# Local attention of a fused transformer kernel: scores as four 32-row products, values stationary, output turned beside the probabilities

## What is computed

```python
xw = x.reshape(B * nw, WINDOW, C)                      # WINDOW = 64, C = 128
qkv = (xw @ W_qkv).reshape(B * nw, WINDOW, 3, NUM_HEADS, HEAD_DIM)
q, k, v = (qkv[:, :, 0], qkv[:, :, 1], qkv[:, :, 2])
q = _layernorm(q, ln_gamma, ln_beta)                   # over the 8 features of a head
k = _layernorm(k, ln_gamma, ln_beta)
attn = jnp.einsum('bqhd,bkhd->bhqk', q * SCALE, k)     # per window and head
attn = jax.nn.softmax(attn, axis=-1)
out = jnp.einsum('bhqk,bkhd->bqhd', attn, v).reshape(B * nw, WINDOW, C)
out = out @ W_proj + b_proj
...
x = x + _L1_attn_ref(_layernorm(x, axis=-1), L1_attn_W_qkv, ...)
```

## Time and profile before

| | us |
|---|---|
| three runs | 891.72, 892.42, 892.43 |
| median | 892.42 |
| the profiled execution | 885.71 |
| its span, first to last instruction | 883.9 |
| attention stage in it, first score product to the next stage's first product | 161.4 to 323.1 |
| mean granted clock of TensorE over the span | 0.903 of full |

### The profile page before, as it was taken

One profiled execution on the slowest core, in us unless ns is written; L12 is line 12 of the kernel. 1 busy time (PEld: TensorE's weight loads), 2 busy tenths in 40 slices (PEclk: granted clock), 3 DMA queues, 4 the chain that ended last, 5 costly groups with the idle time before them and its releaser, 6 DMA issues. The chain is left out here.

```text
span 883.9 us, 11015 instructions
## 1 busy us (share of the span) xinstructions
PE 731.3 (83%) x3306; PEld 469.4 (53%) x3306; DVE 686.8 (78%) x1615; ACT 570.6 (65%) x926; POOL 394.5 (45%) x427
## 2 busy tenths in 40 slices
PE   4788998779998889999778988877778767877787
PEld 3666765445555567777566867643223222222565
DVE  6685786798998638777767888968899778786785
ACT  5264664657474435664636767667899879777776
POOL 6638665634345105555329977534323332230330
PEclk9999998988697669999969999987899889789999
DMA  4200000100000000000001000000000000000001
GB/s 134 72 12 13 16 16 18 34 24 25 13 25 19 0 1 1 1 1 0 1 0 37 1 1 0 1 0 1 1 0 1 1 1 0 1 0 1 1 1 48
DMA packets 9610, 11.59 MB, mean 13 GB/s; under 512 B 720, under 2 KB 5712, under 8 KB 9552
## 3 DMA queue, kind: packets, MB, share of 16 engines
q1 hardware_dynamic: 9552, 10.89, 4.3%
HBM read 9.84 MB, written 1.05 MB: 12 GB/s over the span
## 5 line engine op out<-in xcount | busy, mean ns | idle before, releaser
L1032 POOL TENSOR_TENSOR rbuf<-B,rbuf 128x512 fp32r<-128x512 f32 x96 | 124.1, 1295 | 83.6 <-ACT rbuf L960 83.4
L497 POOL TENSOR_SCALAR small<-small 128x4 f32<-128x4 f32 x32 | 8.5, 265 | 173.3 <-DVE small L387 172.8
L994 DVE TENSOR_TENSOR B<-B,up_banks 128x512 f32<-128x512 f32 x68 | 46.4, 683 | 42.3 <-PE up_banks L733 25.8
L945 ACT ACTIVATE B<-gate_banks 128x512 f32<-128x512 f32 x68 | 40.6, 599 | 59.4 <-PE gate_banks L733 58.3
L960 ACT ACTIVATE rbuf<-B 128x512 fp32r<-128x512 f32 x100 | 62.5, 625 | 17.3 <-DVE B L1010 12.3
L1010 DVE TENSOR_TENSOR B<-B,spread_bank 128x512 f32<-128x512 f32 x96 | 64.7, 678 | 11.0 <-ACT B L949 7.0
L1757 ACT ACTIVATE B<-B,VEC 128x1024 f32<-128x1024 f32 x48 | 55.3, 1151 | 22.4 <-DVE B L1752 22.3
L731 PE MATMUL gate_banks<-XH,WH 128*128 128x512 f32 x152 | 67.0, 441 | 0.8 <-ACT YT L1355 0.8
L733 PE MATMUL gate_banks<-XH,WL 128*128 128x512 f32 x152 | 62.4, 410 | 0.0
L732 PE MATMUL gate_banks<-XL,WH 128*128 128x512 f32 x152 | 62.3, 410 | 0.0
L949 ACT ACTIVATE B<-gate_banks,WR 128x512 f32<-128x512 f32 x64 | 44.0, 689 | 27.3 <-PE gate_banks L733 26.7
(11 more groups left out here) (347 smaller groups left out, 2274.3 us busy)
## 6 DMA issues: line engine op xcount, KB each, us to landing
STG<-in_w_split SPq DMA_DIRECT2D x27, 256.0 KB, 2.7
X<-in_x SPq DMA_DIRECT2D x4, 256.0 KB, 5.0
out<-X SPq DMA_DIRECT2D x4, 256.0 KB, 2.3
WR<-in_w_raw SPq DMA_DIRECT2D x1, 524.5 KB, 4.4
STG<-in_w_exact SPq DMA_DIRECT2D x2, 256.0 KB, 2.6
STG<-in_w_split SPq DMA_DIRECT2D x5, 64.0 KB, 1.9
STG<-in_w_split SPq DMA_DIRECT2D x1, 192.0 KB, 2.4
STG<-in_w_split SPq DMA_DIRECT2D x1, 128.0 KB, 2.0
```

Of the source, the lines that this page charges most:

```text
L994: nc.vector.tensor_tensor(MO[n % 2], AO[n % 2], U[n % 2][:, :], ALU.mult).then_inc(mul_done, 1)
L1032: e_.tensor_tensor(lo, hidden(f, n), hi.bitcast(F32), ALU.subtract).then_inc(hl_ready, 1)
```

## The change

Scores. The keys are no longer masked per tile and head. A product now reads 32 partitions, that is four heads, with keys of which each of four copies keeps every fourth head; so 4 copies (`KM`, four slots of 512 columns) serve a whole chunk, made once a chunk by `attn_keys`, which also applies gain and offset (slots 0 and 1 on ScalarE, 2 and 3 on GpSimd). A unit's scores are four products of 32 rows, 64 columns of weights and 256 streaming columns, into two banks.

Turned probabilities go back into the same two banks as the unit's scores. So the scores of unit N+1 wait for the copy-out of unit N-1.

Weighing. The values are the weights (18 columns), the turned probabilities stream (64 columns), eight products a unit, each pair of heads at its own 32 output partitions. The result comes out features by tokens; ScalarE copies it (`copy_out`), TensorE turns it by two transposes of 64 rows into free columns of the probabilities' banks (`turn_out`), and the copy-out of a later unit, widened from 512 to 640 columns, takes it along. `finish` reads it from SBUF, now once a unit.

Normalising the heads. The variances are computed with tokens on the partitions (line 1172 of the new file, eight products), root and reciprocal are of 128 x 128, ScalarE spreads them over the features (`attn_spread_act`), and TensorE turns them by full 128-row products (line 1186).

Order. TensorE now does turn(N-1) with turn_out(N-3), weigh(N-2), scores(N+1); ScalarE copy-out(N-1), copy_out(N-2), exp(N). The scores of units 0 and 1 stand inside the last feed-forward block ahead of the stage, before its last two summing triples. `body_start` is gone from the stage.

```diff
-                    i = nc.tensor.matmul(G[u][w * WIN:(w + 1) * WIN, :], QN[c_ % 2][:, tok],
-                                         KM[tile % 2][:, HU * u:HU * u + HU, w * WIN:(w + 1) * WIN],
-                                         start=True, stop=True)
...
+            if N >= 2:
+                pe.wait_ge(pt_ready, N - 1)
...
+            for w in range(2):
+                tok = slice(i_ * P + w * WIN, i_ * P + (w + 1) * WIN)
+                for k in range(2):
+                    rows = slice(32 * (2 * u + k), 32 * (2 * u + k) + 32)
+                    i = nc.tensor.matmul(SB2[u][w * WIN:(w + 1) * WIN, k, :], QN[c % 2][rows, tok],
+                                         KM[c % 2][rows, :, tok], start=True, stop=True)
...
+        def attn_keys(eng, c):
...
+            eng.wait_ge(qk_read, 2 * c + 1)
...
+            for j in ((0, 1) if eng is nc.scalar else (2, 3)):
+                dst = KM[c % 2][:, j, :]
+                if eng is nc.scalar:
+                    i = eng.activation(dst, kc, ACT.Identity, scale=key_g[:, j:j + 1], bias=key_b[:, j:j + 1])
+                else:
+                    i = eng.tensor_scalar(dst, kc, key_g[:, j:j + 1], key_b[:, j:j + 1], ALU.mult, ALU.add)
...
+            def turn_out(M):
+                u = M % 2
+                pe.wait_ge(o_copied, M + 1)
+                for k in range(2):
+                    rows = slice(64 * k, 64 * k + 64)
+                    i = nc.tensor.transpose(SBW[u][:, k, HALF:TURN_W], OT[u][rows, :], ident[rows, rows])
+                i.then_inc(o_turned, 1)
...
-                    i = nc.tensor.matmul(SP[:, pr * 36:(pr + 1) * 36], PT[u][:, q * P:(q + 1) * P],
-                                         VB[:, tile % TL, pr, :, :, :].rearrange("p a b d -> p (a b d)"),
-                                         start=True, stop=True)
...
+                        i = nc.tensor.matmul(SP[32 * q:32 * q + 2 * (HD + 1), u * P + w * WIN:u * P + (w + 1) * WIN],
+                                             VB[:, tile % TL, 4 * u + q, w, :, :].rearrange("p h d -> p (h d)"),
+                                             PT[u][:, q // 2, at_:at_ + WIN], start=True, stop=True)
...
+                a.wait_ge(o_full, N - 1)
...
+                nc.scalar.activation(PT[N % 2], SBW[N % 2][:, :, 0:TURN_W], ACT.Copy).then_inc(pt_ready, 1)
...
+            def copy_out(N):
+                u = N % 2
+                a.wait_ge(o_full, N + 1)
...
+                nc.scalar.activation(OT[u], SP[:, u * P:(u + 1) * P], ACT.Copy).then_inc(o_copied, 1)
...
             for n in range(UN):
                 N = c * UN + n
-                probs(N)
                 if N:
                     evac(N - 1)
+                if N >= 2:
+                    copy_out(N - 2)
+                probs(N)
...
+                    if f is FFN0 and at_ == (NC - 1, f.blocks - 3):
+                        for N in range(2):
+                            attn_scores(pe, N)
```

More of the change, by code:

```diff
@@ L659, in later_weights @@
         def later_weights(g, chain):
+            for row, dst in (("ln_g1", key_g), ("ln_b1", key_b)):
+                i = nc.gpsimd.tensor_scalar(dst, raw("head_of_4"), raw(row), 1.0, ALU.mult, ALU.mult)
+            chain(i)
             WM32 = buf[11]
@@ L1230, in attn_mask @@
-        def attn_mask(eng, tile):
-            c, i_ = tile // TL, tile % TL
-            if tile >= NC * TL:
-                return
-            heads, done = {nc.vector: (range(0, 8), masked_dve), nc.gpsimd: (range(8, 12), masked_pool),
-                           nc.scalar: (range(12, 16), masked_act)}[eng]
-            eng.wait_ge(qk_ready, 2 * c + 1)
-            if tile >= 2:
-                eng.wait_ge(s_full, 2 * (tile - 2) + (1 if eng is nc.vector else 2))
-            for h in heads:
-                dst, src = KM[tile % 2][:, h, :], KN[c % 2][:, i_ * P:(i_ + 1) * P]
+            if step in (4, 5):
+                k, x = step - 4, (kc, qc)[step - 4]
+                v.wait_ge(rstd_full, 2 * c + k + 1)
+                v.wait_ge(centred, 2 * c + 2)
+                nc.vector.tensor_tensor(x, x, R[:, :], ALU.mult).then_inc(qk_read, 1)
@@ new lines, in attn_prepare_dve @@
+            if step == 5:
+                v.wait_ge(qk_read, 2 * c + 2)
+                if c >= 2:
+                    v.wait_ge(s_full, UN * (c - 1))
+                nc.vector.tensor_scalar(QN[c % 2], qc, raw("ln_g1"), raw("ln_b1"), ALU.mult, ALU.add)\
+                    .then_inc(qk_ready, 1)
+        def attn_keys(eng, c):
+            if c >= NC:
+                return
+            eng.wait_ge(qk_read, 2 * c + 1)
+            if c >= 2:
+                eng.wait_ge(s_full, UN * (c - 1))
+            elif c == 1:
+                eng.wait_ge(yt_ready, count(2, 0))
+            for j in ((0, 1) if eng is nc.scalar else (2, 3)):
+                dst = KM[c % 2][:, j, :]
@@ L1360, in attn_project_dve @@
                 v.wait_ge(y_full, count_y(2, c))
+            else:
+                v.wait_ge(yt_ready, count(2, 0))
             nc.vector.tensor_copy(rbuf[0][:, :], A32w).then_inc(ah_ready, 1)
@@ L1452, in attn_dve @@
                     hook(-1)
-                attn_hooks(n, c, hook, 7)
-                if n == 5 and nxt:
-                    attn_prepare_dve(v, c + 1, 2)
+                attn_hooks(n, c, hook, 6)
+                if N >= 4:
+                    finish(N - 4)
             if not nxt:
-                finish(NU // 2 - 2)
-                finish(NU // 2 - 1)
+                for M in range(NU - 4, NU):
+                    finish(M)
                 attn_project_dve(v, c)
```

270 lines of the change are left out of this document (147 added, 123 removed).

## The result

The changed kernel takes 900.88 us (median of 4 runs, 899.31 to 902.42), the kernel before 892.31 (891.72 to 892.43): 1.0097 times, 95% interval 1.0079 to 1.0115. It is slower, where 0.7% less was forecast; 900.88 lies inside the range that the prediction gave, 870 to 903, but on the other side of no change. The profiled executions lie further apart, 900.86 against 885.71 us (spans 898.9 and 883.9): the one of before was quick for its kernel. What follows splits the 15.0 us of the two spans; the medians lie 8.6 apart.

A forecast was written before the change was run, and what follows sets the result against it. TensorE and its granted clock were taken to bound the kernel, VectorE close behind. Three chunks +4, last chunk -6, head -2.5, tail -2 sum to -6.5 us: 879.2 in profile time, forecast 886 against 892.4, range 870 to 903.

The forecast's parts named there:

- Product prices: TensorE's work per attention unit: 1.95 us against 2.46 at the upper clock level, about 3.2 against 4.7 at the lower.
- no concurrency: Rival: 18-column products run one after another, weighing takes 1.8 us, +1.1 a unit; 920 us, chance 0.06.
- The new chain: From exp to exp through turn, copy-out and result copy: 2.65 us a unit at the upper level, 3.4 at the lower.
- Side work and the lower level: Per-chunk preparation on the path: 10.5 us upper, 18 lower; whole chunk 31.7 and 45.2 against 34.2 and 48.1.
- Which clock: Attention stage's share of time at the lower level, chosen 55% against 38% now: 37.9 us a chunk, +4 for three.
- Last chunk: The last attention chunk prepares nothing, so the cheaper unit shows: 27 to 33 us against 39.9, counted as only -6.
- Head: Start of attention: scores inside the feed-forward tail wait for GpSimd's keys; -2.5 us (bounds -4 and +2), first exp near 161.5.
- Tail: From the last exp to the output's turn: 5.3 us instead of 7.5, counted as -2.
- the clock falls and stays: Rival: lower level for 85% of the stage, chunk 42.5 us, +8 in all; 900 us, chance 0.22.
- the rows argument: In the attention units, TensorE work drops by a fifth and score rows to a quarter, while the period falls by less.
- The clock holds: Rival: lower-level share stays at 38%, giving 878 us, or 860 wholly at the upper level; under 880, chance 0.22.
- hidden anyway: Rival: ScalarE's cycle takes what TensorE gives, chunks stay at 36.6 us, only the ends move; 888 to 893, chance 0.10.

The follow-up runs named there:

- e10: e7_head with each of a unit's four score products reading all 128 partitions instead of 32 (scores not the reference's); 0.9902 times the kernel before.
- e7_head: Changed kernel with values read at n=1, the projection's split ahead of the preparation step, and GpSimd's chunk 0 keys early; 0.9861 times the kernel before.
- e14_head_again: The kernel of e7_head run once more, unchanged; 0.9920 times the kernel before.
- e8_again: The changed kernel itself run once more, unchanged; 1.0066 times the kernel before.
- e2_values: Changed kernel with ScalarE's read of the value rows moved from unit n=0 back to n=1; 0.9999 times the kernel before.
- e3_valproj: e2_values with VectorE's split of the projection also put ahead of the preparation step at n=4; 0.9954 times the kernel before.
- e1_rows32: Kernel before with every score product reading only the first 32 of 128 partitions (scores not the reference's); 929.99 us, 1.0452 times the kernel before.
- e13_masked_queries: e7_head with VectorE's spread products and ScalarE's keys later, and 128-row scores from chunk 1 by queries zeroed outside 32 channels; 0.9913 times the kernel before.

## Why the prediction was wrong

**What bounds the kernel.** Right that TensorE and its clock decide. But in the changed kernel waits between queues decide as much, and for them the sum has no term.

**Product prices.** Right. Scores 0.68 us to the next start (forecast 0.5 plus a change of shape), turn back 0.21 (0.26), weighing 0.42 (0.45), all of a unit 1.9 (1.95) and 3.0 at the lower level (3.2). The two 32-row products of different row groups do run side by side, with the two halves: all four in 0.66 us, where e10's two by two take 1.09. The rule of the Trainium skill, "TensorEngine Tiling (Array Packing)", section "Tiling Modes", that a change of mode drains the engine, costs at most the 0.2 us a unit that the sum held for it: the parts of the unit in the rows above add up to 1.9 us with nothing between them but the wait for ScalarE. With that the rival "no concurrency", which had the weighing at 1.8 us, is out.

**The new chain.** Right in kind: ScalarE's copy-out releases the scores, unit 2.43 us for 2.65.

**Side work and the lower level.** Windows 1 and 2 of the changed kernel (48.21 us at 0.54, 45.42 at 0.59, so 92% and 82% at the lower level) solve to 30.7 us a chunk at the upper level and 50.7 at the lower, the upper one far out from two chunks that stand mostly low. Forecast were 31.7 and 45.2. The kernel with the waits mended shows which part was wrong: its chunk 1, 36.30 us at 0.81 in e7_head and 41.56 at 0.62 in e14_head_again, solves to 32.2 and 45.8, close to the forecast. So units and side work were priced rightly, and what the lower level lacks is the waits, of which the values' alone is 2.8 us there. The part on ScalarE, "it loses 20.0 us of masks and gains keys", priced what each instruction takes, and passed over that L1244's move to n=0 puts it ahead of a weighing that TensorE issues in the next iteration.

**Which clock.** This is the term that failed, together with the waits that the sum left out. "Between 38% and 90% I choose 55%" came out at 72, 92 and 74% in chunks 0 to 2 (between exps, from 0.64, 0.54 and 0.63; 72, 76 and 70% in e8_again). Three chunks cost +16.2 us instead of +4 (165.50 to 294.26 against 164.00 to 276.58). An estimate with the forecast's own prices parts the two: at the measured shares they give 43.7 and 40.7 us for chunks 1 and 2, forecast were 37.9 each, and measured are 48.5 and 44.3. So some 8.5 us are the share, and 8.4 what the prices left out, the waits first; chunk 0 took 2.0 less than forecast. Over the three chunks the share is 80% in the changed kernel (73% in e8_again), and in the mended ones 55% (e2_values), 61% (e3_valproj), 55% (e7_head) and 74% (e14_head_again). So the 55% was tolerable for a kernel without the new waits, though not in each execution, and wrong for this one. What the rows do to the clock is shown by e1_rows32; what the waits do to it, beyond their own length, is not settled (e2_values).

**Last chunk.** -6 forecast, -5.6 measured (27.9 against 33.5 us between first and last exp), and -3.5 in e8_again (30.0).

**Head.** -2.5 forecast with +2 as the upper bound, +1.5 measured (+0.3 in e8_again, first exp at 164.33). It counted that keys of "1.3 to 5 us" would be waited for, but not who is behind the wait: two summing triples, and through them `YT` and the first exp. With the keys early the first exp comes at 158.94, 2.6 us better than the 161.5 forecast.

**Tail.** -2 forecast; from the last exp to the output's turn 4.92 us (322.18 to 327.10) against 7.51: -2.6.

**Behind the stage.** Nothing was forecast. From the next stage's first product to the end the changed kernel's trace is 5.5 us longer (566.3 against 560.8); its first 20 us stand at a clock of 0.79 against 0.92, which by estimate is some 2.5 of them. The rest stays open, and is no more than executions differ by there: from the last exp to the end e7_head took 573.0 us and its repeat 575.2, the changed kernel 576.7 and e8_again 575.6, the kernel before 573.8. With this term the five add up: 16.2 - 5.6 + 1.5 - 2.6 + 5.5 = 15.0 us.

**The rivals.** The one that ends slower, "the clock falls and stays" at 85%, gave 900 us; measured 900.9. The nearness is in part luck: it had +18 for the three chunks (16.2 measured), -6 for the last (-5.6) and -4 for the ends (-1.1), nothing behind the stage (+5.5), and so 893.7 in the profile's time, where 900.9 was measured too. Its place was only half right: it named units 6, 7, 0 and 1 as plain units, and unit 0 it was, but by the values' wait. It had a chance of 0.22 and should have had more: e1_rows32 shows that the rows argument, listed there "for it", costs some 40 us alone. "The clock holds" (0.22) and "hidden anyway" (0.10) are out by the stage's 0.64 and its 156.7 us. "TensorE waits at a chunk's start for GpSimd's keys" was named as what would make the prediction wrong, and did.

## What to carry to other kernels

Price a row-tiled product twice: by its length, which falls with concurrency, and by the granted clock of the stretch around it, which fell with the rows in use; copies masked to full rows brought it back here, though not the time (e13_masked_queries). When an instruction is moved in a queue, look up which iteration issues what it waits for, and who stands behind it: here one placement and one order of keys were worth 0.7% or more each, and turned a gain into a loss. And do not judge a saved wait by its unit alone, but by unit and clock together: late steps gave nothing (0.992, as e7_head's repeat) where the level was low and won (0.979 after 0.990) where it held. Compare such units only at one level, and a kernel's clock only over several executions.

## What the runs showed that was not expected

- Score products of 32 rows instead of 128, with their number, columns and order unchanged, take the stage from 0.81 to 0.57 and the kernel 4.5% up; 64 rows do nearly the same (0.61, 3.8%).
- Products of 128 rows of which three quarters carry zeros hold the clock: 0.92, 0.91 and 0.87 in chunks 1 to 3 of e13_masked_queries, beside 0.64 in its chunk 0.
- The same instructions met a clock of 0.81 in one execution's chunk 1 and 0.62 in another's, 36.3 and 41.6 us.
